# Second attention: four output blocks of the finished head pair placed among the score groups and value products

## The chip, the cores and the metric

The kernel runs on one core of a Trainium2 chip. The metric is the device time of one execution in microseconds; each number is the median of several runs. The core has five engines that work side by side: TensorE (matmuls, called PE in the profile, with its weight loads as PEld), VectorE (DVE), ScalarE (ACT), GpSimd (POOL) and SyncE (SP), which only issues transfers here. They meet at semaphores.

## The reference

Four layers are applied to x (8 batches of 128 tokens, 512 wide), each behind a layer norm and added to x. The third is the one that matters here:

```
q = rope(query @ Wq), 32 heads of 128;  k = rope(key @ Wk), v = value @ Wv, 8 heads of 128
logits = 30 * tanh((q . k) * 0.0884 / 30), masked
weights = softmax(logits)
attn = weights . v              (128 tokens x 4096 for each batch)
x = x + attn @ Wo               (512 wide)
```

Query is the normed x, key and value are the context. Before it come a cross attention with 32 heads and a gated feed-forward of width 1376, behind it a linear layer with LoRA.

## The kernel before

The work is in float32. Large products are made as three products of halves: `product` gives w_lo x_hi, w_hi x_lo and w_hi x_hi, where "hi" is a rounded copy (made by ScalarE) and "lo" the rest (made by VectorE or GpSimd). Score products and turns (transposes) are plain float32 matmuls, which appear as two instructions for each score block.

`grouped_attention_phase` is the second attention. It goes through 16 head pairs p = 4r + u, in 4 rounds r of 4 blocks u. The first and the last round are written out, the two between them are a loop. A block p does the projections, rope and scores of pair p, and finishes pair p-1: turn of the softmax weights, value product, output product. So 15 of the 16 blocks have an output. In the grouping used here:

- a projection is 12 matmuls 512 wide (four chunks by three); a block has four for Q, and two more for K where u is 0 or 2;
- the scores of a pair come in four groups j (two batches by two heads), group j in PSUM bank 4 + j;
- `turn(p-1, j)` puts the turned weights into the same bank 4 + j, `pv(p-1, j, ...)` the value product, also in this bank. From there ScalarE makes the high half of the attended values (`attn_hi`) and VectorE the low half (`attn_lo`). `scores(p, j)` waits for `attn_lo` of quarter j, since it writes over the bank;
- `output_batch(r, u, b)` multiplies the attended values of batch b by the output weights: 6 matmuls 512 wide into one of banks 0 to 3. It waits for quarter b // 2 of the low half, and for its bank: the fourth last group of banks 0 to 3 must have been read. VectorE's `output(r, u, b)` adds the bank to the residual and frees it;
- where u is 0, `values(r)` follows, the value projection for four pairs.

The order on each engine is written out by hand. TensorE's order in a block is, before the change: K projections if any, Q 0 to 2, turns 0 and 1, Q 3, value 0, turn 2, value 1, turn 3, scores 0, value 2, scores 1, value 3, scores 2, scores 3, outputs 0 to 7. ScalarE goes through the swaps for the rope, `attn_hi` and `probs_hi`, the high halves of the next Q weights (and K weights), the softmax `tanhs` and `exps`, and last the high half of the output weights, which waits for output 7. VectorE does the low halves, then the softmax steps (`logits`, `inverse`) with the output additions between them. GpSimd does the rope's sine product, the low halves of weights and `normalise`.

In the last block VectorE also splits the LoRA matrices (`lora.split_ab_lo`), right after the addition numbered 5. It needs two transfers that wait for score group 3 of that block, and ScalarE's `lora.split_ab_hi`, which stands behind the softmax. The fold of the LoRA matrices follows on TensorE right behind the outputs, and then the turns and value products of the last pair.

Of the kernel before, what the change touches and what calls it, by code (L numbers as in the profile page):

```python
# [24 lines left out]
B = 8  # L25
# [27 lines left out]
def product(pe, out, w, x, start, stop):  # L53

    pe.matmul(out, w[1], x[0], start=start, stop=False)  # L55
    pe.matmul(out, w[0], x[1], start=False, stop=False)  # L56
    return pe.matmul(out, w[0], x[0], start=False, stop=stop)  # L57


def tok(b, n=1):  # L60
    return slice(b * P, (b + n) * P)
# [1077 lines left out]
def grouped_attention_phase(core, io, weights_early, norm_row, lora):  # L1139
# [9 lines left out]
    with ExitStack() as ctx:  # L1149
# [65 lines left out]
        def seq(r, u, at):  # L1215


            if is_first(r, u) and at < OUT_AT[0]:
                return at
            return PER * r - 8 + at  # L1220

        def seq_out(r, u, n):
            return PER * r - 8 + (OUT_AT[u] if not (isinstance(r, int) and r == ROUNDS) else DC) + n

        def out_bank(r, u, n):
            return ((0 if isinstance(r, int) and r == ROUNDS else OUT_AT[u]) + n) % PROJ_BANKS
# [9 lines left out]
        def rope_of(r, u, slot, half):  # L1236

            return ROPES * r + ROPE_AT[u] + (2 if u in K_AT else 0) + 2 * half + slot
# [5 lines left out]
        def nth_quarter(p, j, back=0):  # L1244

            n = 4 * (p - back) + j + 1
            return None if isinstance(n, int) and n <= 0 else n
# [20 lines left out]
        with nc.Block() as block:  # L1268
# [29 lines left out]
            @block.tensor  # L1298
            def _(pe):
                def bank_free(s):  # L1300
                    if not isinstance(s, int) or s >= PROJ_BANKS:
                        pe.wait_ge(proj_free, s - PROJ_BANKS + 1)

                def weights_ready(kind, n):
                    pe.wait_ge(w_hi[kind], n + 1)
                    pe.wait_ge(w_lo[kind], n + 1)

                def project(s, at, kind, slot, half):

                    src = cT if kind == "K" else xT  # L1310
                    bank_free(s)
                    for c in range(DC):
                        col = (slot * DC + c) * P
                        mm = product(pe, banks[:, at % PROJ_BANKS, :], [w[:, col:col + P] for w in wt[kind]],
                                     [x[:, c, half * HALF:(half + 1) * HALF] for x in src], c == 0, c == DC - 1)
                    mm.then_inc(proj_ready, 1)

                def values(r):
                    weights_ready("V", r)
                    for n in range(4):  # L1320
                        s = seq(r, 0, V_AT + n)
                        bank_free(s)
                        for t in range(2):
                            for c in range(DC):
                                mm = product(pe, banks[:, (V_AT + n) % PROJ_BANKS, t * 256:(t + 1) * 256],
                                             [x[:, c, tok(2 * n + t)] for x in cT],
                                             [w[:, c * 256:(c + 1) * 256] for w in wt["V"]], c == 0, c == DC - 1)
                        mm.then_inc(proj_ready, 1)

                def scores(p, j, rope, first):  # L1330
                    pe.wait_ge(rope_done, rope + 1)
                    if not first:
                        pe.wait_ge(att_lo, nth_quarter(p, j, 1))
                    for t in range(4):
                        b, h = 2 * j + t // 2, t % 2
                        mm = pe.matmul(banks[:, QUARTER_BANK + j, tok(t)], q[:, h, tok(b)], k_[:, tok(b)],
                                       start=True, stop=True)
                    mm.then_inc(scores_ready, 1)

                def turn(p, j):  # L1340
                    pe.wait_ge(probs_ready, nth_quarter(p, j))
                    for t in range(4):
                        mm = pe.transpose(banks[:, QUARTER_BANK + j, tok(t)], probs[:, 4 * j + t, :], ident[:, :])
                    mm.then_inc(turned, 1)

                def pv(p, j, kv):
                    pe.wait_ge(pT_lo, nth_quarter(p, j))
                    for t in range(2):
                        mm = product(pe, banks[:, QUARTER_BANK + j, tok(2 * t, 2)], [s[:, 2 * j + t, tok(kv)] for s in v],
                                     [s[:, tok(2 * t, 2)] for s in pT[j % 2]], True, True)  # L1350
                    mm.then_inc(pv_ready, 1)

                def output(r, u):

                    weights_ready("O", 4 * r + u - 1)
                    for b in range(B):
                        output_batch(r, u, b)

                def output_batch(r, u, b):
                    if b % 2 == 0:  # L1360
                        pe.wait_ge(att_lo, nth_quarter(4 * r + u, b // 2, 1))
                    bank_free(seq_out(r, u, b))
                    for h in range(2):
                        mm = product(pe, banks[:, out_bank(r, u, b), :], [x[:, h, tok(b)] for x in att],
                                     [w[:, h * D:(h + 1) * D] for w in wt["O"]], h == 0, h == 1)
                    mm.then_inc(proj_ready, 1)

                def body(r, u, first, last):
                    p = 4 * r + u
                    before_kv = (u - 1) // 2 % 2  # L1370
                    if u in K_AT:
                        weights_ready("K", 2 * r + u // 2)
                        for half in range(2):
                            project(seq(r, u, K_AT[u] + half), K_AT[u] + half, "K", 0, half)
                    weights_ready("Q", p)
                    for n in range(4):
                        if n == 3 and not first:
                            turn(p - 1, 0)
                            turn(p - 1, 1)
                        project(seq(r, u, Q_AT[u] + n), Q_AT[u] + n, "Q", n % 2, n // 2)  # L1380
                    if not first:

                        pe.wait_ge(proj_free, seq(r, 0, V_AT + 3) - (PER if u == 0 else 0) + 1)
                        pv(p - 1, 0, before_kv)
                        turn(p - 1, 2)
                        pv(p - 1, 1, before_kv)
                        turn(p - 1, 3)
                    scores(p, 0, rope_of(r, u, 1, 0), first)
                    if not first:
                        pv(p - 1, 2, before_kv)  # L1390
                    scores(p, 1, rope_of(r, u, 1, 0), first)
                    if not first:
                        pv(p - 1, 3, before_kv)
                    scores(p, 2, rope_of(r, u, 1, 1), first)
                    scores(p, 3, rope_of(r, u, 1, 1), first)
                    if not first:
                        output(r, u)
                    if u == 0:
                        values(r)

                loop(pe, body)
                lora.fold(pe, FOLD, proj_ready, bank_free)
                tail = PAIRS - 1
                turn(tail, 0)
                turn(tail, 1)
                pv(tail, 0, 1)
                turn(tail, 2)
                pv(tail, 1, 1)
                turn(tail, 3)
                pv(tail, 2, 1)  # L1410
                pv(tail, 3, 1)
                weights_ready("O", PAIRS - 1)
                norm.weave_tensor(pe, lambda b: output_batch(ROUNDS, 0, b))
# [108 lines left out]
            def _(dve):  # L1522
# [44 lines left out]
                def body(r, u, first, last):  # L1567
                    p = 4 * r + u
# [27 lines left out]
                        attn_lo(p - 1, 3)  # L1596

                    done = 0
                    for step, j, outs in ((logits, 0, 0), (logits, 1, 1), (logits, 2, 1), (inverse, 0, 0), (logits, 3, 1),
                                          (inverse, 1, 1), (inverse, 2, 1), (inverse, 3, 3)):  # L1600
                        step(p, j)
                        for _ in range(outs):
                            if not first:
                                output(r, u, done)
                            if last and done == 5:
                                lora.split_ab_lo(dve)
                            done = done + 1
# [290 lines left out]
```

## Time and profile before

| | |
|---|---|
| median of 3 runs | 1780.58 us (1779.57 to 1781.34) |
| the profiled execution | 1781.57 us, span 1779.8 us |
| granted TensorE clock over the span | 0.988 |
| busy: TensorE, VectorE, GpSimd, ScalarE | 95%, 53%, 39%, 35% |
| the 15 blocks with an output | 1163.9 to 1718.2 us of the span |

Times in the rows are microseconds from the span's start, unless ns is written. In a timeline the second number is the duration, and a bracket tells the idle time of the engine ahead of the instruction and what ended it. The matmuls are pipelined: one starts before the record of the one ahead of it has ended, so that costs are read from start to start. Names of buffers can be those of another stage, since buffers are shared: wtV holds the output weights of the second attention, wtO its Q weights, wtB its K weights and, in its other part, the turned softmax weights of odd quarters. L55 to L57 are the three lines of `product`, L1336 is a score product, L1343 a turn, L1552 a low half, L1530 the logits, L1564 the addition of an output.

### The profile page before, as it was taken

The numbers are of one execution on the slowest core, as the hardware profiler recorded it, in microseconds if no ns is written. First come the engines' busy times: TensorE is split into PE (matmuls) and PEld (weight loads), VectorE is DVE, ScalarE is ACT, GpSimd is POOL, SyncE is SP. The second block draws the span as 40 slices with busy tenths as digits, with TensorE's granted clock in tenths as the row PEclk, the third lists the DMA queues.
The fourth block names the chain that finished last, engine by engine and source line by source line (L and its number), as shares of the span: only waits on it lengthen the run. The fifth ranks groups of instructions, "written<-read, shape, count | busy, mean of one in ns | idle before, by whom it ended". The sixth has DMA issues, their size and how long they took to land. (4 is left out here: it accounts for less than half of the span.)

```text
span 1779.8 us, 26198 instructions
## 1 busy us (share of the span) xinstructions
PE 1690.8 (95%) x9412; PEld 1455.2 (82%) x9412; DVE 935.0 (53%) x1483; ACT 631.2 (35%) x1739; POOL 698.0 (39%) x493
## 2 busy tenths in 40 slices
PE   3999999999999999999989999799999999999997
PEld 2888888888888888888868886688888788888875
DVE  6745444355444354444453445656656555665574
ACT  2223322133322133322232222455545445554550
POOL 5434333244333344333344333444435434443424
PEclk9999999999999999999989999899999999999998
DMA  4110111110111110111011110201011110010011
GB/s 166 57 51 1 50 50 50 50 50 0 50 50 50 50 50 0 50 50 55 2 36 54 54 37 24 64 30 36 30 36 42 44 36 30 24 42 25 13 48 48
DMA packets 30616, 75.03 MB, mean 42 GB/s; under 512 B 5745, under 2 KB 10225, under 8 KB 30545
## 3 DMA queue, kind: packets, MB, share of 16 engines
q1 hardware_dynamic: 30544, 74.10, 12.0%
q8 instruction: 43, 0.70, 0.2%
q14 instruction: 29, 0.23, 0.0%
HBM read 71.99 MB, written 2.10 MB: 42 GB/s over the span
## 5 line engine op out<-in xcount | busy, mean ns | idle before, releaser
L1654 POOL TENSOR_TENSOR g_swapped<-g_swapped,rawB 128x512 f32<-128x512 f32 x80 | 103.7, 1296 | 162.9 <-ACT g_swapped L1438 162.9
L858 POOL TENSOR_TENSOR wtV_lo<-rawV,wtV_hi 128x1024 fp32r<-128x1024 f32 x15 | 36.1, 2409 | 320.3 <-ACT wtV_hi L690 320.3
L678 ACT COPY x_pT<-banks 128x512 f32<-128x512 f32 x64 | 37.5, 586 | 348.0 <-PE banks L588 348.0
L55 PE MATMUL banks<-wtV_hi,cT_lo 128*128 128x256 f32 x512 | 144.9, 283 | 0.0
L57 PE MATMUL banks<-wtV_hi,cT_hi 128*128 128x256 f32 x512 | 144.8, 283 | 0.0
L56 PE MATMUL banks<-wtV_lo,cT_hi 128*128 128x256 f32 x512 | 144.7, 283 | 0.0
L872 POOL TENSOR_TENSOR x_probs<-x_probs,x_inv 128x512 f32<-128x512 f32 x64 | 66.8, 1044 | 163.5 <-DVE x_inv L754 160.7
L670 ACT ACTIVATE x_probs<-x_probs,x_top 128x128 f32<-128x128 f32 x256 | 99.2, 389 | 38.2 <-DVE x_top L745 38.2
L762 DVE COPY x_v<-banks 128x512 f32<-128x512 f32 x64 | 44.0, 690 | 127.7 <-PE banks L57 127.7
L762 DVE COPY x_k<-banks 128x512 f32<-128x512 f32 x64 | 44.1, 691 | 124.9 <-PE banks L57 124.9
L1543 DVE TENSOR_TENSOR normed<-banks,rawB 128x512 f32<-128x512 f32 x80 | 55.3, 692 | 96.3 <-ACT g_swapped L1438 96.3
L781 DVE TENSOR_TENSOR resid<-banks,resid 128x512 f32<-128x512 f32 x128 | 84.0, 686 | 40.0 <-PE banks L57 40.0
L55 PE MATMUL banks<-wtO_hi,x_att_lo 128*128 128x512 f32 x256 | 102.9, 402 | 0.7 <-DVE x_att_lo L757 0.7
L55 PE MATMUL banks<-wtV_hi,g_att_lo 128*128 128x512 f32 x256 | 102.6, 401 | 0.0
L57 PE MATMUL banks<-wtV_hi,g_att_hi 128*128 128x512 f32 x256 | 101.1, 395 | 0.0
L56 PE MATMUL banks<-wtV_lo,g_att_hi 128*128 128x512 f32 x256 | 101.1, 395 | 0.0
L57 PE MATMUL banks<-wtO_hi,x_att_hi 128*128 128x512 f32 x256 | 101.1, 395 | 0.0
L55 PE MATMUL banks<-xT_hi,wtO_lo 128*128 128x512 f32 x256 | 101.0, 395 | 0.0
L56 PE MATMUL banks<-wtO_lo,x_att_hi 128*128 128x512 f32 x256 | 101.0, 394 | 0.0
L57 PE MATMUL banks<-xT_hi,wtO_hi 128*128 128x512 f32 x256 | 99.8, 390 | 0.0
L56 PE MATMUL banks<-xT_lo,wtO_hi 128*128 128x512 f32 x256 | 99.8, 390 | 0.0
L56 PEld LDWEIGHTS banks<-wtV_lo,cT_hi 128*128 128x128 f32 x512 | 98.1, 192 | 0.7
(212 smaller groups left out, 4983.1 us busy)
## 6 DMA issues: line engine op xcount, KB each, us to landing
rawA<-in_x_wA SPq DMA_DIRECT2D x16, 512.0 KB, 6.1
rawV<-in_x_wV SPq DMA_DIRECT2D x16, 512.0 KB, 3.9
rawB<-in_x_wB SPq DMA_DIRECT2D x16, 512.0 KB, 4.7
rawO<-in_x_wO SPq DMA_DIRECT2D x16, 512.0 KB, 5.8
rawO<-in_g_wQ SPq DMA_DIRECT2D x16, 512.0 KB, 3.3
rawV<-in_g_wO SPq DMA_DIRECT2D x16, 512.0 KB, 3.3
rawA<-in_f_gu SPq DMA_DIRECT2D x5, 512.0 KB, 3.4
rawB<-in_f_gu SPq DMA_DIRECT2D x5, 512.0 KB, 3.2
```

The source lines that it names most:

```text
L55: pe.matmul(out, w[1], x[0], start=start, stop=False)
L56: pe.matmul(out, w[0], x[1], start=False, stop=False)
L57: return pe.matmul(out, w[0], x[0], start=False, stop=stop)
L670: e = nc.scalar.activation(probs[:, b, :], probs[:, b, :], ACT.Exp, bias=top[:, b:b + 1], accum_out=total[:, b:b + 1])
L678: nc.scalar.copy(pT[:, j, :], banks[:, TURN_BANK + j, :]).then_inc(pT_ready, 1)
L762: dve.tensor_copy(dst, banks[:, bank, :]).then_inc(proj_free, 1)
L781: dve.tensor_tensor(resid[:, b, :], banks[:, b % PROJ_BANKS, :], resid[:, b, :], ALU.add)\
L858: pool.tensor_tensor(wt[kind][1][:, :], raw[kind][:, :], f32(wt[kind][0][:, :]), ALU.subtract)\
L872: pool.tensor_tensor(probs[:, part, :], probs[:, part, :], rows, ALU.mult).then_inc(probs_ready, 1)
L1543: dve.tensor_tensor(out, bank, wide(cos), ALU.mult).then_inc(proj_free, 1)
L1654: pool.tensor_tensor(part, part, sin[:, :].unsqueeze(1).to_broadcast([P, HB, P]), ALU.mult)\
```

## The change

TensorE's order in a block becomes: as before up to turn 3, then output 0, value 2, scores 0, value 3, output 1, scores 1, output 2, scores 2, output 3, scores 3, outputs 4 to 7. VectorE takes the additions up earlier by one: one of them follows logits 0, and only two follow inverse 3. Since the addition numbered 5 now follows inverse 2, VectorE's split of the LoRA matrices comes ahead of inverse 3 in the last block. The first block, which has no output, keeps its order. No work is added or removed.

```
-                def output(r, u):
-
-                    weights_ready("O", 4 * r + u - 1)
-                    for b in range(B):
-                        output_batch(r, u, b)
-
...
                         turn(p - 1, 3)
+                        weights_ready("O", p - 1)
+                        output_batch(r, u, 0)
+                        pv(p - 1, 2, before_kv)
                     scores(p, 0, rope_of(r, u, 1, 0), first)
                     if not first:
-                        pv(p - 1, 2, before_kv)
-                    scores(p, 1, rope_of(r, u, 1, 0), first)
-                    if not first:
                         pv(p - 1, 3, before_kv)
-                    scores(p, 2, rope_of(r, u, 1, 1), first)
-                    scores(p, 3, rope_of(r, u, 1, 1), first)
-                    if not first:
-                        output(r, u)
+                        output_batch(r, u, 1)
+                    for j in range(1, 4):
+                        scores(p, j, rope_of(r, u, 1, j // 2), first)
+                        if not first and j < 3:
+                            output_batch(r, u, j + 1)
+                    if not first:
+                        for b in range(4, B):
+                            output_batch(r, u, b)
...
                     done = 0
-                    for step, j, outs in ((logits, 0, 0), (logits, 1, 1), (logits, 2, 1), (inverse, 0, 0), (logits, 3, 1),
-                                          (inverse, 1, 1), (inverse, 2, 1), (inverse, 3, 3)):
+                    for step, j, outs in ((logits, 0, 1), (logits, 1, 1), (logits, 2, 1), (inverse, 0, 0), (logits, 3, 1),
+                                          (inverse, 1, 1), (inverse, 2, 1), (inverse, 3, 2)):
```

## Rows read from the trace of the kernel before

**Rows 1.** The page, its first part: busy time and share of the span.

```profile
PE 1690.8 (95%) x9412; PEld 1455.2 (82%) x9412; DVE 935.0 (53%) x1483; ACT 631.2 (35%) x1739; POOL 698.0 (39%) x493
```

**Rows 2.** Waits of TensorE, 1163.89 to 1718.21: us in total, times, longest.

```profile
PE banks L1336 <- DVE g_att_lo L1552: 16.2, 30, 0.8
PE banks L55 <- DVE resid L1564: 0.8, 1, 0.8
```

**Rows 3.** Busy time by stretch: length, PE, PEld, DVE, ACT, POOL, clock, DMA share, GB/s.

```profile
1163.89:1718.21 554.32, 537.34 (x2978) 460.53 (x2977) 339.42 (x523) 295.76 (x860) 244.00 (x171) 1.00 0.10 34
```

**Rows 4.** Timeline of TensorE in one block (u = 1), 1329 to 1346.

```profile
1329.00 1.13 PE L1336 MATMUL banks<-g_k,g_q 128*128 128x128 f32 x8 [0.47 <-DVE g_att_lo L1552]
1329.88 0.36 PE L55 MATMUL banks<-g_pT_hi,g_v_lo 128*128 128x256 f32 x1
1330.08 0.28 PE L56 MATMUL banks<-g_pT_lo,g_v_hi 128*128 128x256 f32 x1
...
1330.79 1.13 PE L1336 MATMUL banks<-g_k,g_q 128*128 128x128 f32 x8
1331.68 0.36 PE L55 MATMUL banks<-wtB_hi,g_v_lo 128*128 128x256 f32 x1
...
1332.48 1.05 PE L1336 MATMUL banks<-g_k,g_q 128*128 128x128 f32 x8
1334.13 1.13 PE L1336 MATMUL banks<-g_k,g_q 128*128 128x128 f32 x8 [0.60 <-DVE g_att_lo L1552]
1335.02 0.48 PE L55 MATMUL banks<-wtV_hi,g_att_lo 128*128 128x512 f32 x1
1335.34 0.39 PE L56 MATMUL banks<-wtV_lo,g_att_hi 128*128 128x512 f32 x1
...
1346.30 0.40 PE L55 MATMUL banks<-cT_hi,wtB_lo 128*128 128x512 f32 x1
```

**Rows 5.** Timelines of VectorE, GpSimd and ScalarE in the same block.

```profile
1334.28 2.40 POOL L1642 TENSOR_TENSOR wtO_lo<-rawO,wtO_hi 128x1024 fp32r<-128x1024 f32 x1 [5.40 <-ACT wtO_hi L1459]
1334.74 3.15 DVE L1530 SCALAR_TENSOR_TENSOR g_probs<-g_probs,g_cap,rawB 128x512 f32<-128x512 f32 x2 [0.75 <-ACT g_probs L1422]
1337.26 0.31 ACT L1428 ACTIVATE g_probs<-g_probs 128x128 f32<-128x128 f32 x1 [2.07 <-DVE g_probs L1530]
...
1339.06 0.75 DVE L1530 SCALAR_TENSOR_TENSOR g_probs<-g_probs,g_cap,rawB 128x512 f32<-128x512 f32 x1 [0.57 <-ACT g_probs L1422]
1340.57 1.04 POOL L1648 TENSOR_TENSOR g_probs<-g_probs,g_inv 128x512 f32<-128x512 f32 x1 [3.89 <-DVE g_inv L1535]
```

**Rows 6.** Timeline of TensorE in the last norm: an output block and the next turn.

```profile
1734.52 0.48 PE L55 MATMUL banks<-wtV_hi,g_att_lo 128*128 128x512 f32 x1
...
1736.00 0.60 PE L202 MATMUL banks<-ident,normed 128*128 128x128 f32 x4
```

**Rows 7.** Timelines of TensorE and GpSimd in a block that splits a K weight.

```profile
1366.48 1.13 PE L1336 MATMUL banks<-g_k,g_q 128*128 128x128 f32 x8 [0.47 <-DVE g_att_lo L1552]
...
1371.77 2.39 POOL L1642 TENSOR_TENSOR wtO_lo<-rawO,wtO_hi 128x1024 fp32r<-128x1024 f32 x1 [5.40 <-ACT wtO_hi L1459]
1374.11 1.74 POOL L1642 TENSOR_TENSOR wtB_lo<-rawB,wtB_hi 128x512 fp32r<-128x512 f32 x1
```

**Rows 8.** Timelines at the end of the last block: transfer, split, fold.

```profile
1707.59 1.26 SPq L1723 DMA_DIRECT2D g_swapped<-in_l_b  x1
...
1717.38 0.69 DVE L1738 TENSOR_TENSOR l_b_lo<-rawB,l_b_hi 128x512 fp32r<-128x512 f32 x1
...
1718.21 0.41 PE L55 MATMUL banks<-l_b_hi,l_a_lo 128*128 128x512 f32 x1
```

**Rows 9.** Transfers by issue, 1690 to 1745: size, us to landing.

```profile
g_swapped<-in_l_b SPq DMA_DIRECT2D x1, 256.0 KB, 3.7
```

**Rows 10.** Busy time by stretch around the last norm; columns as in rows 3.

```profile
1740.00:1747.00 7.00, 3.36 (x18) 2.28 (x18) 7.00 (x15) 1.75 (x3) 5.42 (x9) 0.98 0.00 0
1747.00:1757.26 10.26, 7.11 (x20) 5.33 (x21) 4.01 (x8) 1.17 (x2) 6.31 (x7) 0.51 0.00 0
```

More of the change, by code:

```diff
@@ L1387, in body @@
                         turn(p - 1, 3)
+                        weights_ready("O", p - 1)
+                        output_batch(r, u, 0)
+                        pv(p - 1, 2, before_kv)
                     scores(p, 0, rope_of(r, u, 1, 0), first)
                     if not first:
-                        pv(p - 1, 2, before_kv)
-                    scores(p, 1, rope_of(r, u, 1, 0), first)
-                    if not first:
-                        pv(p - 1, 3, before_kv)
-                    scores(p, 2, rope_of(r, u, 1, 1), first)
-                    scores(p, 3, rope_of(r, u, 1, 1), first)
-                    if not first:
-                        output(r, u)
+                        pv(p - 1, 3, before_kv)
+                        output_batch(r, u, 1)
[3 more added lines that the diff above has]
+                            output_batch(r, u, j + 1)
+                    if not first:
+                        for b in range(4, B):
+                            output_batch(r, u, b)
                     if u == 0:
```

## The prediction

> **What bounds the kernel now.** I read the page first: TensorE is busy for 1690.8 of 1779.8 us and no other engine for more than 53% of the span [rows 1]. The reader should conclude that time can only come from gaps and slow steps of TensorE. The profiled execution took 1781.57 us, 1.77 us more than its span, and lies 0.99 us above the median of 1780.58 us; I make the sum against the profiled execution and take the same difference off the median.
>
> Next come the waits of TensorE, cut to the 15 blocks of the second attention that have an output (1163.89 to 1718.21 us). There are only two lines: the score products wait for the low half of the attended values, 30 times, 16.2 us together, and one wait of 0.8 us for a residual sum [rows 2]. The granted clock is 1.00 in that window, the 2.4 GHz level, so nothing there is a clock matter [rows 3]. Thirty waits in 15 blocks is two each. The timeline of one block shows where [rows 4]: one ahead of score group 0 (1329.00, wait A) and one ahead of score group 3 (1334.13, wait B). The other blocks repeat the pattern; no wait of that line is longer than 0.8 us [rows 2].
>
> I cost everything from start to start, because the duration of a matmul reaches into the next one.
>
> **What is in one block now** [rows 4]. A score group takes 1329.88-1329.00 = 0.88. A value product takes 1332.48-1331.68 = 0.80 behind a score group: its first step is 1330.08-1329.88 = 0.20, the other five 0.12. Behind a score group the first 512-wide step is 0.32 as well (1335.34-1335.02), the later ones 0.233. So a step from a narrow group to a product of split halves costs 0.08 more; I call this the changeover. Group 1 starts at 1330.79, 0.91 after value product 2 instead of 0.80: a small wait of 0.11. Groups 2 and 3 start 1334.13-1332.48 = 1.65 apart instead of 0.88, so wait B is 0.77. Eight output blocks take 1346.30-1335.02 = 11.28, that is 0.08 + 8 x 1.40. In total 17.30 us from group 0 to the next block's first projection.
>
> **The change part by part.**
>
> *Wait A.* It stays. Output block 0 takes group 0's place and waits for the same quarter 0 of the attended values. What ended the wait is VectorE's subtraction [rows 4], which follows ScalarE's copy of value product 0. Nothing in the diff is ahead of that. I count a gain of 0.
>
> *Waits B and the 0.11.* Group 3 needs the low half of quarter 3. After the change two output blocks, groups 1 and 2 and a third output block stand between value product 3 and group 3. They cover 1.40+0.88+1.48+0.88+1.48 = 6.1 us, where the way from value product 3 to group 3 takes 1.65. Both waits go: 0.88 us.
>
> *Changeovers.* Before, the stretch has three: value products 2 and 3 and the output. After, it has five: output 0 (behind the turn), value product 3, outputs 2, 3 and 4. (Output 1 stands behind a value product.) Two more at 0.08 is 0.16. That small blocks between 512-wide ones cost no more than this is shown by the last norm, where one output block and one turn of four blocks alternate: 1734.52 to 1736.00 is 1.48 = 1.40 + 0.08 [rows 6].
>
> *Sum of a block*, from the start of output 0: output 0 1.48, values 2 0.72 (behind wide work, no changeover), group 0 0.88, values 3 0.80, output 1 1.40, group 1 0.88, output 2 1.48, group 2 0.88, output 3 1.48, group 3 0.88, outputs 4 to 7 5.68: 16.56 us instead of 17.30. Gain 0.74 us (by the parts 0.88 less 0.16 is 0.72; the rest is rounding).
>
> *What becomes late.* The 0.74 holds only if the banks come free. Outputs 4 to 7 reuse the banks of outputs 0 to 3, which VectorE adds to the residual in its order: logits 0, add 0, logits 1, add 1, logits 2, add 2, inverse 0, logits 3, add 3. I follow the block at 1329.00, with an add as 0.65 us behind the step ahead of it (as the 0.69 us subtraction over as many columns in rows 8), the four exponentials of a group as 4 x 0.3 [rows 5], and a tanh as 0.55, an estimate a little under that subtraction. Value product 3 ends 0.39 later than now (3.87 behind the start instead of 3.48), and ScalarE's last copy of the quarters and its weight split move with it. GpSimd's half of the split follows, 1334.28 to 1336.68 now, 1334.7 to 1337.1 then. VectorE's logits are held by it: the pair takes 3.15 us beside GpSimd, one alone 0.75, and ScalarE's first exponential starts at 1337.26, 0.58 after GpSimd's end [rows 5]. So logits 0 end near 1337.7, add 0 at 1338.3, add 1 at 1339.5, add 2 at 1340.8. Logits 3 wait for group 3 (1339.87) and its tanh, to 1340.7, and end at 1341.6 alone, at 1342.6 behind a normalisation of GpSimd of 1.04; add 3 ends at 1343.3 at the latest. TensorE wants these banks at 1339.9, 1341.4, 1342.8 and 1344.2. The smallest margin is 0.9 us.
> In the six blocks that also split a K weight, GpSimd works from 1371.77 to 1375.85 [rows 7], 0.4 later then. By the same steps add 0 ends at 1375.8 (wanted 1366.48+10.87 = 1377.35), add 1 at 1377.4 (1378.8), add 2 at 1378.7 (1380.2), add 3 at 1380.9 to 1381.2 (1381.6). The smallest margin is 0.4 us. I take no wait, and keep as the bound 0.6 us in each of the six blocks.
> The next block finds its banks free: add 4 ends at 1344.0 and the next projection wants it at 1345.55. The softmax has to be ready only for the next block's first turn, behind three projections. The output weights of the last pair are complete long before: their split on GpSimd ends soon after the block that used the previous ones.
>
> The Trainium skill (SBUF — State Buffer, Who interferes with whom) says that VectorE and GpSimd take a shared port pair as an exclusive lock for a whole instruction. By that rule too, the trace agrees: VectorE finishes its first logits 0.58 us after GpSimd ends. If every added logits step met a whole GpSimd operation, this would be the second rival below.
>
> *The last block* (the 15th). The loads of the LoRA matrices wait for group 3. The second is issued at 1707.59 [rows 8] and takes 3.7 us to land [rows 9]. This block's group 0 starts at 1718.21-17.30 = 1700.91 and group 3 ends at 1700.91+6.02 = 1706.93; after the change it ends at 1700.91+10.87 = 1711.78, 4.85 later. So the load is issued at 1712.45 and lands near 1716.15. Also, VectorE's split of the matrices comes behind its sixth add, and that add now stands ahead of inverse 3: the split comes before inverse 3 and adds 6 and 7. Now its last subtraction ends at 1718.07 [rows 8]. Then the chain starts when the load lands: ScalarE's copy, its second copy beside VectorE's first subtraction, and the second subtraction, about 0.7 us each (0.69 the last): 1716.15 to about 1718.25. TensorE is through its outputs at 1700.91+16.56 = 1717.47 and starts the fold at about 1718.35, now 1718.21 [rows 8]. Folds 2 and 3 need adds 6 and 7 at 1719.1 and 1719.7, as they are wanted. So this block gives nothing, and loses about 0.1 us. Without the late load it would give 0.74; with a landing 1 us later it would lose 1.1.
>
> *Sum.* 14 x 0.74 - 0.1 = 10.3 us. 1781.57 - 10.3 = 1771.3 for such an execution, 1780.58 - 10.3 = **1770.3 us** for the median, 0.58% less.
>
> *Clock behind it.* The granted clock is 0.51 (the 1.2 GHz level) from 1747.0 to 1757.26, at the end of the last norm, in which TensorE was busy for 3.36 of 7 us [rows 10]; before and after it is full. In that stretch 7.11 us of matmuls run, which at 2.4 GHz would take half as long at best, so at most 3.6 us hang on where it lies. Everything there moves by 10 us and the clock may fall and rise at another place of the work. I take 0; the three runs before lie within 1.8 us of each other, which holds this too, and I keep 2 both ways.
>
> **The rivals.**
> 1. *The forecast as above*, 1768 to 1773 us: 0.74.
> 2. *The bank waits bite* (faster, by less). The logits now stand one by one between the adds, and each can meet GpSimd. If add 3 is 1.0 us later than I reckon in every block, output 7 waits 0.6 in six and 0.1 in eight: the gain is 0.74 x 14 - 6 x 0.6 - 8 x 0.1 - 0.1, about 5.9 us: 1774.7. For it: margins of only 0.4 us and 3.15 us for a pair of logits. Against it: inverse 0 has to come first for the normalisation, and there is just one such meeting. 0.12.
> 3. *Small groups between wide ones cost more than the changeover* (no change, or slower). The stretch gets nine borders between output blocks and the narrower work instead of one. If each of the eight added ones costs 0.11 us (0.88/8), the waits that go are paid back; at the 0.20 us that the whole first step behind a score group takes (1330.08-1329.88), a block loses 1.60-0.88 = 0.72 us, 10 us over 14: 1791. Against it stands the alternation in the last norm, where both borders together cost 0.08 [rows 6]. 0.05 for no change (1777 to 1784), 0.03 for slower.
> 4. *Outputs 4 to 7 wait for the softmax order* (slower): logits 2 and 3 wait for score groups that come 4.9 us later than now. The point from which it decides is VectorE 0.9+0.74 = 1.64 us later than I reckon in every block; at 3 us later it would be 1780.6 + 14 x 1.36 = 1799.6. VectorE's and ScalarE's busy time, 339 and 296 of 554 us, speaks against it [rows 3]. 0.03.
> 5. *Wait A shrinks too* (faster still): it would need the chain of the first value product to be earlier, and no row shows how. Its idle time is 16.2 us less 15 times the 0.60 of wait B, 7.2 us [rows 2, 4]: 1763 at best. 0.03.
>
> **The numbers.** A difference of 0.2% (3.6 us) is about what a measurement of this kernel can tell from none. The likeliest is 1770.3. Its own bounds are the clock, 2 both ways, and on the slow side 0.6 x 6 = 3.6 for the K blocks. Range 1768.0 to 1774.8: it leaves out part of case 2, and cases 3 to 5. Faster by over 0.2%: 0.74+0.12+0.03 = 0.89. Within: 0.05 and a little of case 4, 0.06. Slower: 0.05.
>
> **What the profile of the changed kernel would show.** Right: in the waits of TensorE one line of 15 waits for the attended values' low half, now ahead of an output product, about 7 us in all; no wait ahead of score groups; from output 0 to the next projection 16.5 us. Right for the last block: a wait of about 0.9 us ahead of the fold, released by the split of the LoRA matrices. Wrong: waits for the residual (adds) ahead of outputs 4 to 7, most likely output 7 in blocks with a K weight (case 2 or 4); or a first output matmul whose next starts later than 0.32 us, or narrow groups above 0.88 (case 3).

## The result and the profile after

The changed kernel takes 1768.29 us (median of 4 runs, 1766.66 to 1769.13); the kernel before, beside it on the same chip, takes 1780.07 (1779.39 to 1781.34). The ratio is 0.9932, interval 0.9915 to 0.9949. It is faster by 11.8 us where 10.3 were forecast. The direction was right and the gain was sized too small: the time lies at the low edge of the range, and the ratio times 1780.07 is 1767.97, just under it. The profiled executions, 1781.57 before and 1768.79 after, differ by 12.8 us.

The page of the changed kernel, its first part (columns as in [rows 1]):

```profile
PE 1683.6 (95%) x9412; PEld 1453.4 (82%) x9412; DVE 932.9 (53%) x1483; ACT 632.7 (36%) x1739; POOL 697.8 (39%) x493
```

The waits of TensorE in the changed kernel from 1164 to 1706 us, the same 15 blocks as in [rows 2]:

```profile
PE banks L55 <- DVE g_att_lo L1550: 8.7, 15, 0.9
PE banks L55 <- DVE resid L1562: 1.6, 1, 1.6
PE banks L55 <- DVE l_b_lo L1736: 0.4, 1, 0.4
```

Fifteen waits for the attended values are left of thirty, and they stand ahead of a product (L55), output block 0. No score group waits. The residual sum is named once in the whole stretch: not at an output block, where a bank wait would stand, but between the two passes of the loop.

Busy time of those blocks (columns as in [rows 3]):

```profile
1164.63:1705.48 540.85, 530.13 (x2978) 458.79 (x2976) 337.00 (x523) 297.38 (x861) 242.40 (x170) 1.00 0.10 35
```

The stretch is 554.32 - 540.85 = 13.47 us shorter. It begins 0.74 later than before, behind code that is the same in both kernels, and what follows it takes 61.52 instead of 61.59 us: that makes the 12.8 of the span. So the clock behind the stretch, which the forecast took as 0 with 2 both ways, cost and gave nothing.

TensorE in the block of [rows 4], which now begins with output 0 at 1325.81:

```profile
1325.81 0.50 PE L55 MATMUL banks<-wtV_hi,g_att_lo 128*128 128x512 f32 x1 [0.57 <-DVE g_att_lo L1550]
...
1327.31 0.28 PE L55 MATMUL banks<-g_pT_hi,g_v_lo 128*128 128x256 f32 x1
...
1328.03 1.06 PE L1336 MATMUL banks<-g_k,g_q 128*128 128x128 f32 x8
1328.84 0.36 PE L55 MATMUL banks<-wtB_hi,g_v_lo 128*128 128x256 f32 x1
...
1329.63 0.39 PE L55 MATMUL banks<-wtV_hi,g_att_lo 128*128 128x512 f32 x1
...
1331.02 1.06 PE L1336 MATMUL banks<-g_k,g_q 128*128 128x128 f32 x8
...
1335.58 1.06 PE L1336 MATMUL banks<-g_k,g_q 128*128 128x128 f32 x8
1336.39 0.48 PE L55 MATMUL banks<-wtV_hi,g_att_lo 128*128 128x512 f32 x1
...
1342.05 0.39 PE L55 MATMUL banks<-cT_hi,wtB_lo 128*128 128x512 f32 x1
```

Read from start to start: output 0 1.50, value product 2 0.72, group 0 0.81, value product 3 0.79, output 1 1.39, group 3 0.81, outputs 4 to 7 5.66. From the first output to the next projection it is 16.24 us; 16.56 was forecast and 17.30 [rows 4] was the time before. The other blocks repeat it, at 16.20 to 16.25, but for the one at the loop's jump and the last one, which are told below. All terms agree with the forecast to 0.02 except the score groups, which I had at 0.88. The weight loads, which TensorE does ahead of each matmul, point at why. The first weight load of this group 0 in the changed kernel, and of groups 0 and 2 in the kernel before (matmuls at 1329.00 and 1332.48 [rows 4]):

```profile
1327.91 0.98 PEld L1336 LDWEIGHTS banks<-g_k,g_q 128*128 128x128 f32 x8
```

```profile
1328.97 0.97 PEld L1336 LDWEIGHTS banks<-g_k,g_q 128*128 128x128 f32 x8 [0.68 <-issue]
...
1332.36 0.98 PEld L1336 LDWEIGHTS banks<-g_k,g_q 128*128 128x128 f32 x8
```

Ahead of a group that nothing holds, the load starts 0.12 us before the matmul; at the wait it starts 0.03 before. The 0.88 was read from the group behind wait A. I read the 0.07 as the part of the first load that the wait leaves uncovered; that it comes with the wait is shown below, that it is the load is argued from these starts.

VectorE in the changed kernel, the same block:

```profile
1331.89 2.48 DVE L1528 SCALAR_TENSOR_TENSOR g_probs<-g_probs,g_cap,rawB 128x512 f32<-128x512 f32 x1 [0.75 <-ACT g_probs L1420]
1334.30 0.68 DVE L1562 TENSOR_TENSOR resid<-banks,resid 128x512 f32<-128x512 f32 x1
...
1339.23 0.68 DVE L1562 TENSOR_TENSOR resid<-banks,resid 128x512 f32<-128x512 f32 x1
```

The first logits are held for 2.48 us beside GpSimd's split of a weight, as forecast, and then the additions run: number 0 ends at 1334.98 and number 3 at 1339.91, where output 7 starts at 1340.65. The margin of 0.7 us, thinner than the 0.9 forecast, is enough. In the K block from 1362.31 the smallest is 1.2 (addition 1 ends at 1373.19, output 5 starts at 1374.36), where 0.4 was forecast.

### The profile page after: what moved, and what is told of

Read it like the earlier page. It is cut to its first block and busy times, and to the rows that moved or that the text cites. A ratio compares the mean times of both kernels' runs of the same rounds, so it can differ in the third digit from the quotient of the medians.

```text
span 1767.0 us, 26198 instructions
## 1 busy us (share of the span) xinstructions
PE 1683.6 (95%) x9412; PEld 1453.4 (82%) x9412; DVE 932.9 (53%) x1483; ACT 632.7 (36%) x1739; POOL 697.8 (39%) x493
## 5 line engine op out<-in xcount | busy, mean ns | idle before, releaser
L55 PE MATMUL banks<-wtV_hi,cT_lo 128*128 128x256 f32 x512 | 144.9, 283 | 0.0
L55 PE MATMUL banks<-wtV_hi,g_att_lo 128*128 128x512 f32 x256 | 106.1, 415 | 8.7 <-DVE g_att_lo L1550 8.7
L55 PE MATMUL banks<-wtO_hi,x_att_lo 128*128 128x512 f32 x256 | 102.8, 402 | 0.7 <-DVE x_att_lo L757 0.7
L55 PE MATMUL banks<-xT_hi,wtO_lo 128*128 128x512 f32 x256 | 100.9, 394 | 0.0
```

## The experiments

Times are medians beside runs of the kernel before on the same chip, except where a kernel named is the base of the edit. "Stretch" is from the first of output 0 and group 0 to the next block's first projection; "wait A" is the time from the start of turn 3 to that start, less the 0.35 that a turn takes when the next step follows at once.

**One half at a time.** TensorE's new order alone, with the additions in the old order:

```
-  ((logits, 0, 1), ..., (inverse, 3, 2))
+  ((logits, 0, 0), ..., (inverse, 3, 3))
```

> TensorE's new order with VectorE's additions in the old order (add 0 behind logits 1, three behind inverse 3). Theory (covered waits are the whole gain, provided the banks come free in time): in the changed kernel add 3 ends 1.4 us ahead of output 7's wish in a block of u = 1; in the old order add 2 takes its place in time and add 3 follows inverse 1, so output 6 waits about 0.8 us in every block, more where a K weight is split. The time is 1776 to 1780 us, and TensorE's waits show a line of about 14 waits for the residual sum ahead of outputs. Rival (VectorE's order does not matter, there is enough slack): 1768.3 us, no such line.

It took 1777.9 us, ratio 0.9987 [0.9978, 0.9996], inside what was expected. The waits of its TensorE, 1140 to 1722 us, then its VectorE and its TensorE in the same block:

```profile
PE banks L55 <- DVE g_att_lo L1550: 8.8, 15, 0.9
PE banks L55 <- DVE resid L1562: 6.7, 11, 1.6
```

```profile
1332.13 3.15 DVE L1528 SCALAR_TENSOR_TENSOR g_probs<-g_probs,g_cap,rawB 128x512 f32<-128x512 f32 x2 [0.75 <-ACT g_probs L1420]
1335.20 0.68 DVE L1562 TENSOR_TENSOR resid<-banks,resid 128x512 f32<-128x512 f32 x1
...
1338.10 1.45 DVE L1528 SCALAR_TENSOR_TENSOR g_probs<-g_probs,g_cap,rawB 128x512 f32<-128x512 f32 x1 [0.22 <-ACT g_probs L1420]
1339.47 0.68 DVE L1562 TENSOR_TENSOR resid<-banks,resid 128x512 f32<-128x512 f32 x1
```

```profile
1340.21 0.50 PE L55 MATMUL banks<-wtV_hi,g_att_lo 128*128 128x512 f32 x1 [0.55 <-DVE resid L1562]
```

Behind a pair of logits addition 0 comes at 1335.20 instead of 1334.30 (0.65 later, counted from the start of output 0), and addition 2 now stands behind the fourth logits: it ends at 1340.15, 2.4 us later than in the changed kernel by the same count, and output 6 starts at 1340.21. The residual sum is waited for eleven times (about 14 were expected), one of them the gap at the loop's jump. Outside that block and the last the stretch is 16.59 to 17.09 instead of 16.22. In four of the K blocks, those with 16.60, the view lists no wait, but the timeline has one of 0.35 ahead of output 4: group 3 takes 1.16 instead of 0.81 to the matmul at 1374.33, where addition 0 ends at 1374.27. So the place of the additions on VectorE decides over four fifths of the gain: 2.1 of 11.8 us are left. Part of the loss is the fold of the last block, which waits 1.1 us here.

VectorE's new order alone, on the kernel before:

> The kernel before with VectorE's additions in the new order alone. Theory: nothing TensorE waits for in the 14 ordinary blocks changes, 1780.1 us plus or minus 1, with wait A and wait B as before (30 waits, 16.2 us); in the last block the LoRA split can only come earlier or stay. Rival (part of the gain comes from the earlier additions): 1776 us or less.

1779.03 us, ratio 0.9997 [0.9988, 1.0006], the 30 waits of 16.2 us unchanged. Worth nothing by itself; of the 1 us between the medians the trace shows 0.46 in the block at the loop's jump.

**How many outputs.** Only outputs 0 and 1 moved, ahead of groups 2 and 3, with VectorE's new order:

```
   scores(p, 0, ...); pv(p - 1, 2, ...); scores(p, 1, ...); pv(p - 1, 3, ...)
+  output_batch(r, u, 0)
   scores(p, 2, ...)
+  output_batch(r, u, 1)
   scores(p, 3, ...)
-  output(r, u)
+  for b in range(2, B): output_batch(r, u, b)
```

> Only outputs 0 and 1 stand among the score groups, one ahead of group 2 and one ahead of group 3; groups 0 and 1 and value products 2 and 3 as before. Theory (a score group costs 0.88 us behind a wait and 0.81 behind running work, wait A costs 0.10 more ahead of an output than ahead of a group): the stretch from group 0 to the next projection is 0.88+0.80+0.11+0.88+0.80+1.40+0.81+1.48+0.81+8.48 = 16.45 us, wait A is back to 0.65 to 0.73: 0.14 us a block worse than the changed kernel, 1770.3 us. Rival (a score group got cheaper because of the wide product ahead of it, not because the wait is gone): groups 0 and 1 then stay at 0.88 and groups 2 and 3 get 0.81, the same time, but a group directly behind a value product without a wait would show 0.88. Rival (each border between output and group costs): with fewer borders it would be faster than the changed kernel, below 1767.

1767.92 us, ratio 0.993 [0.9916, 0.9944]: the same as with four, and 2.4 us under what I expected. Its TensorE in the block:

```profile
1324.40 1.13 PE L1336 MATMUL banks<-g_k,g_q 128*128 128x128 f32 x8 [0.47 <-DVE g_att_lo L1551]
1325.28 0.36 PE L55 MATMUL banks<-g_pT_hi,g_v_lo 128*128 128x256 f32 x1
...
1326.19 1.13 PE L1336 MATMUL banks<-g_k,g_q 128*128 128x128 f32 x8
...
1329.26 1.06 PE L1336 MATMUL banks<-g_k,g_q 128*128 128x128 f32 x8
1330.07 0.48 PE L55 MATMUL banks<-wtV_hi,g_att_lo 128*128 128x512 f32 x1
```

Group 0, behind its wait, takes 0.88 again, and so does group 1 behind its small wait of 0.11; a group behind an output takes 0.81. Both prices stand in one block. That it is the wait and not the narrow value product ahead shows in the changed kernel, where group 0 stands behind value product 2, unheld, and takes 0.81. The stretch is 16.41 (16.45 expected), 0.2 longer than with four outputs, and wait A is back at 0.72 from 0.82. By the blocks the kernel should be 0.5 us longer than with four outputs, less than the medians can tell: 13 x 0.18 more, 15 x 0.10 less, and 0.4 less in the last block, where the fold does not wait. I had expected 2.0 more, with a stretch a little too long and without that 0.4. So nearly all that the change brings is in getting two outputs in front of group 3.

**Wait A grew.** It was counted as unchanged, but measured 0.76 to 0.82 instead of 0.65 to 0.72 (in two blocks 1.10 and 1.11 instead of 1.00 and 1.02). The subtraction that ends it, in the changed kernel:

```profile
1324.87 0.69 DVE L1550 TENSOR_TENSOR g_att_lo<-banks,g_att_hi 128x512 fp32r<-128x512 f32 x1
```

It ends at 1325.56 and output 0 starts at 1325.81, 0.25 later; group 0 used to start 0.15 behind it. `output_batch` waits for the attended values and then for its bank, a second wait in the queue behind the late one. The two waits exchanged:

```
+  bank_free(seq_out(r, u, b))
   if b % 2 == 0:
       pe.wait_ge(att_lo, ...)
-  bank_free(seq_out(r, u, b))
```

> The changed kernel with the wait for the bank ahead of the wait for the attended values in every output block, so that nothing stands between the late release and the matmul. Theory (wait A grew by 0.10 us because one more semaphore wait stands behind the late one in TensorE's queue): wait A returns to 0.65 to 0.73 start to start, 15 x 0.10 = 1.5 us less, 1766.8 us. Rival (the 0.10 belongs to the weight load of a split product behind a wait): no change, 1768.3 us.

1765.9 us, ratio 0.9923 [0.9909, 0.9936]. The waits of its TensorE, 1140 to 1722:

```profile
PE banks L55 <- DVE g_att_lo L1550: 7.2, 15, 0.8
```

7.2 instead of 8.7 us: 0.10 a block, and output 0 starts 0.15 behind the subtraction again. The time alone could not tell this from the changed kernel, since the intervals of the two ratios overlap; the fifteen blocks of the trace can. The bank had long been free; the wait for it cost 0.10 only because it stood behind the one that came last. The rival, that the 0.10 belongs to the weight load of a split product, fell.

**The last block.** The forecast had it lose 0.1 us because the LoRA matrices arrive late, with a wait of about 0.9 ahead of the fold. It gained 0.5: 16.79 from its first output to the fold, where the kernel before takes 17.30. The fold waits 0.43:

```profile
1705.48 0.51 PE L55 MATMUL banks<-l_b_hi,l_a_lo 128*128 128x512 f32 x1 [0.43 <-DVE l_b_lo L1736]
```

Is it the load at all? Its condition was taken back to one that is met early:

```
-  (scores_ready, 4 * PAIRS)
+  (rope_done, ROPES * ROUNDS)
```

> The changed kernel, but the LoRA matrices' transfers wait for the last rope instead of for score group 3 of the last block, so they start some 8 us earlier. Theory (in the last block the late landing holds the fold by 0.43 us): the wait ahead of the fold goes or falls to 0.1, and the kernel gains 0.3 to 0.45 us, which the times can hardly show: 1767.9 us. Rival (VectorE's split is held by its place in the order or by ScalarE's softmax): the wait stays at 0.4 us.

1768.35 us, ratio 0.9924 [0.9911, 0.9938], the same as the changed kernel. The loads go out some 10 us earlier in the block and the wait stays 0.43: my theory fell. What is late is VectorE. In this kernel, GpSimd's normalisations, VectorE's scaling and the fold:

```profile
1688.83 0.34 SPq L1720 DMA_DIRECT2D g_swapped<-in_l_a  x1
...
1700.90 2.04 POOL L1646 TENSOR_TENSOR g_probs<-g_probs,g_inv 128x512 f32<-128x512 f32 x2 [1.31 <-DVE g_inv L1533]
...
1702.08 1.15 DVE L1732 TENSOR_SCALAR rawB<-g_swapped,l_coef 128x512 f32<-128x512 f32 x1
...
1704.66 0.50 PE L55 MATMUL banks<-l_b_hi,l_a_lo 128*128 128x512 f32 x1 [0.43 <-DVE l_b_lo L1736]
```

The scaling starts beside GpSimd and ends 0.29 after GpSimd's end at 1702.94, 1.15 long. Where it runs alone it takes 0.48: in the kernel before (at 1716.21), and with two outputs, where the fold does not wait. The Trainium skill (SBUF — State Buffer, Who interferes with whom) has VectorE and GpSimd share a port pair under an exclusive lock, which whoever issues first holds for the whole instruction. By that rule the scaling, which starts second, is held until GpSimd is done, which agrees. It does not hold every step of VectorE: the residual addition at 1701.47, which reads one of its operands from a bank, takes its usual 0.69 beside the same GpSimd work.

**Wait A itself.** Its cause was looked for ahead of TensorE: in the ScalarE and VectorE queues the halves of attended quarter 0 stand behind the last rope block's swap and cosine product. They were put ahead of these, with the high and low half of the turned weights of quarter 2:

```
   # ScalarE
+  attn_hi(p - 1, 0); probs_hi(p - 1, 2)     (ahead of the last swap)
   # VectorE
+  attn_lo(p - 1, 0); probs_lo(p - 1, 2)     (ahead of the last rotate_cos)
```

> The changed kernel with the high and low half of value quarter 0 and of turned quarter 2 made ahead of the last swap of the rope, on ScalarE and VectorE. Theory (wait A is the chain: last projection, swap, copy, subtraction): output 0 can start 0.6 us earlier, wait A falls from 0.77-0.82 to about 0.2 us in each of 15 blocks, 9 us: 1759 to 1761 us, if the later rope of the last Q half is in time for score group 2. Rival (it moves the lateness to value products 2 and 3 or to groups 2 and 3): new waits ahead of those, gain under 4 us, 1765 or more.

1758.53 us, ratio 0.9875 [0.986, 0.989], 9.8 us under the changed kernel; in the traces 7.9 of them lie between the first of the stretches and the fold. The output of the same block starts 0.61 behind turn 3: the view names no wait any more, and 0.26 beyond a turn is left of wait A. The stretch is still 16.20 to 16.23:

```profile
1321.34 0.60 PE L1343 MATMUL banks<-ident,g_probs 128*128 128x128 f32 x4
1321.95 0.49 PE L55 MATMUL banks<-wtV_hi,g_att_lo 128*128 128x512 f32 x1
```

The same edit on the kernel before:

> The same reordering of ScalarE and VectorE on the kernel before, where group 0 stands behind wait A. Theory: wait A falls by 0.5 to 0.6 us in 15 blocks as well, but groups 2 and 3 come sooner behind the last rope, which ends 1.3 us later, so part of it can come back there; 1771 to 1776 us. If it gains as much as in the changed kernel, the two waits are independent: 1771. If nothing, wait A only hid behind another limit that the change removed: 1780.

1779.21 us, ratio 0.9991 [0.9982, 1.0]. I had expected 1771 to 1776 and was wrong. Waits of its TensorE, 1140 to 1722, and the score groups of the block:

```profile
PE banks L1336 <- DVE g_att_lo L1553: 12.9, 30, 0.5
```

```profile
1327.02 1.13 PE L1336 MATMUL banks<-g_k,g_q 128*128 128x128 f32 x8
...
1329.32 1.13 PE L1336 MATMUL banks<-g_k,g_q 128*128 128x128 f32 x8 [0.45 <-DVE g_att_lo L1553]
...
1332.65 1.13 PE L1336 MATMUL banks<-g_k,g_q 128*128 128x128 f32 x8 [0.41 <-DVE g_att_lo L1553]
```

Wait A has gone (0.17 is left), but group 1 now waits 0.45 and group 3 0.41: still thirty waits, and the stretch grew from 17.30 to 17.75 or more. Without outputs among the groups, TensorE only meets the next link of the same chain earlier. This is the clearest reading of what the change under study does: it puts independent work, four outputs of 1.4 us in each block, where the chain of the attended values is waited for, and only then is a shorter chain worth anything.

**All of it together**: exchanged waits, early load and the moved halves on the changed kernel.

> The changed kernel with all three: bank wait first, early LoRA transfers, quarter 0 ahead of the last swap. Theory (the three are independent): 1768.3 - 1.5 - 0.4 - 9 = 1757.4 us. Rival (with wait A nearly gone, the bank wait's order has nothing left to give): 1759 us.

1756.91 us, ratio 0.9866 [0.9851, 0.9881], as expected. No wait for the attended values is left in it: output 0 starts 0.17 beyond a turn behind turn 3. To that, VectorE's scaling of LoRA B put ahead of GpSimd's normalisations, behind addition 2:

```
                             if not first:
                                 output(r, u, done)
+                            if last and done == 2:
+                                lora.scale_b(dve)
```

> The version with all three edits, and VectorE's scaling of the LoRA matrix moved behind addition 2 of the last block. Theory (the fold's wait of 0.43 us, which the early transfer alone did not remove, is the scaling held up beside GpSimd's normalisations: 1.15 us instead of 0.48): the wait ahead of the fold falls to 0.1 us or goes, 0.3 to 0.4 us less in the trace, not to be told in the times: 1756.5 us. Rival (ScalarE's copies behind the softmax are the limit): the wait stays above 0.3 us.

1756.49 us, ratio 0.9865 [0.9849, 0.9882], the same. The two VectorE steps in question:

```profile
1687.58 0.48 DVE L1735 TENSOR_SCALAR rawB<-g_swapped,l_coef 128x512 f32<-128x512 f32 x1
...
1691.77 1.40 DVE L1743 TENSOR_TENSOR l_a_lo<-g_swapped,l_a_hi 128x512 fp32r<-128x512 f32 x1
```

The scaling fell to 0.48, and the subtraction of LoRA A, which takes 0.68 in the changed kernel, now meets GpSimd and takes 1.40. The fold's wait went from 0.43 to 0.32, where 0.1 or none was expected: the collision had moved. By its number the rival named there, ScalarE's copies behind the softmax, would have said the same (above 0.3). The trace speaks against it: the copy that this subtraction needs ends at 1691.63, VectorE's own addition ahead of it at 1691.74, and GpSimd works from 1690.58 to 1692.62, so that an earlier copy would have changed little. No run moved that copy.

**The gap at the loop's jump.** In one block the stretch is 17.95 (before: 18.25), and TensorE idles 1.56 us between the last output and the next K projection:

```profile
1411.59 0.49 PE L55 MATMUL banks<-cT_hi,wtB_lo 128*128 128x512 f32 x1 [1.56 <-DVE resid L1562]
```

In the kernel before it was 0.78 at the same place, in the kernel with the three edits 2.06. The releaser shown is VectorE's addition (in the last it is "issue", no releaser at all), but the place is where rounds 1 and 2 meet, the loop's jump. The kernel with the three edits, its two rounds of the loop written out on all engines:

```
-  with engine.Fori(1, ROUNDS - 1) as r:
+  for r in range(1, ROUNDS - 1):
```

> The version with all three edits, with the two middle rounds of the second attention written out instead of looped. Theory (the idle stretch of TensorE between the two passes of the loop, 0.9 us before, 1.7 in the changed kernel, 2.1 to 2.2 with all three, is the jump and not a wait for the residual): it goes, 1.5 to 2.2 us less, 1755 us; the longer program may give some back by code loading. Rival (it is a real wait for VectorE): it stays, 1756.9 us.

1754.51 us, ratio 0.9856 [0.984, 0.9873], the fastest, 25.5 us under the kernel before. TensorE and VectorE at this place:

```profile
1401.44 0.40 PE L57 MATMUL banks<-wtV_hi,g_att_hi 128*128 128x512 f32 x1
1401.68 0.39 PE L55 MATMUL banks<-cT_hi,wtB_lo 128*128 128x512 f32 x1
```

```profile
1401.88 0.69 DVE L1563 TENSOR_TENSOR resid<-banks,resid 128x512 f32<-128x512 f32 x1 [0.36 <-PE banks L57]
```

The projection follows the output by 0.24 us, and starts before VectorE's last addition does. The gap was the jump and not that addition. What sets its size was not tried. From start to start it is 1.18 us before, 1.96 in the changed kernel and 2.46 with the three edits, but how dense the kernel is does not decide: VectorE's new order alone has 0.77, and the kernel with the early scaling, the same as the one with 2.46 but for the last block, has 1.94.

## Why the prediction was right in kind and too small in size

- **Waits B and the 0.11**: right. Both went, in all 15 blocks. The kernel with two outputs shows that the first two are enough.
- **Score groups at 0.88**: mis-sized, the main error, and the step that failed. The sum of a block prices all four groups at 0.88 after their waits are gone. They take 0.81 when not behind a wait, 4 x 0.07 = 0.28 a block; with a few hundredths in the other terms the block gained 1.07, not 0.74. I read the price of a group from those at a wait. [rows 4] does not show the other price from start to start: groups 0, 1 and 3 stand behind a wait, and group 2 is followed by one. But it shows the difference: the record of group 2 is 1.05 long, those of the three held groups 1.13. For the same reason wait B was 0.84 and not 0.77.
- **Changeovers of 0.08**: right. Rival 3, dear borders, fell: the nine borders cost what was counted.
- **Wait A unchanged**: mis-sized by 0.10 a block, 1.5 us in all, on the other side. The chain was unchanged as said, but the instruction at its end now carried a second wait (shown by exchanging the two).
- **Bank waits**: none, as the likeliest case had it. Rivals 2 and 4 fell. That the margin matters, the old order of additions shows: there addition 2 ends 2.4 us later, and ten bank waits come up besides the jump's.
- **Last block**: mis-sized, -0.1 forecast, +0.5 measured. The load landed in 2.9 us instead of the 3.7 taken, and did not matter at all; VectorE's scaling beside GpSimd did, 1.15 us instead of 0.48. The forecast saw that the split moves ahead of inverse 3, but put nothing for its meeting GpSimd there.
- **The jump**, which I had not seen as a thing apart, kept 0.44 of the 0.74 forecast for its block.
- **Rival 5, wait A shrinks too**: it did not by itself. "No row shows how" looked at rows alone: the order of the ScalarE and VectorE queues in the code shows how, and with it changed the kernel took 1758.53.

Put together from the blocks of the two traces: 13 x 1.07 for the stretches, 0.30 for the block at the jump, 0.51 for the last, less 15 x 0.10 for wait A is 13.2 us, where the stretch of 15 blocks measures 13.47. The forecast's 10.3 by the same list lacks 4.3 of the stretches (3.6 of it the score groups) and 0.6 of the last block, and is too generous by 1.5 for wait A and 0.4 for the jump. That it came within 1.5 us of the median's 11.8 is in part luck, since errors on both sides cancel and the traces differ by 0.7 us ahead of the blocks.

## What to carry to other kernels

Price a narrow group of matmuls from an instance that nothing holds, and look at its weight load beside it: behind a wait it led by 0.03 us instead of 0.12. Put the semaphore that is reached last in the last place ahead of an instruction. Two moves that each seem to remove a wait need not add up: find out whether independent work stands in the gap first, since shortening the chain alone (1779.21) was worth nothing, and with outputs among the groups 9.8 us.

## What the hardware showed that was not expected

- A group of eight 128-wide float32 matmuls costs 0.88 us from start to start behind a wait and 0.81 otherwise, its first weight load 0.03 and 0.12 us ahead.
- A second semaphore wait, long met, behind one that is met late costs TensorE 0.10 us (8.7 against 7.2 us over 15 blocks).
- At the one jump of this loop TensorE takes 0.77 to 2.46 us from start to start in eleven kernels, shown in the profile as a wait for another engine or as "issue"; written out, it is 0.24, the usual step.
- VectorE steps of 0.48, 0.68 and 0.75 us when alone took 1.15, 1.40 and 2.48 us beside a GpSimd operation. The residual addition, with one operand in a bank, stayed at 0.69 beside one.
